# Graph layers on one core: in the second layer, one tile of rows in sixteen chunks fetched by SP row by row

## Chip, cores and metric

One of the eight cores of a Trainium2 chip runs the whole kernel. The metric is the device time of one execution in microseconds; before the change three runs took 8138.94, 8143.89 and 8145.72 us, median 8143.89 us.

## The reference

Twelve and a half thousand nodes of 128 numbers pass through two graph layers over 400,000 edges that are sorted by destination. The second layer is the one that the change touches:

```python
# layer 2, in the reference's own function _L1_gnn_ref(h, src, dst, etype, norm, W, b):
H = jnp.einsum('ni,rio->rno', h, W)
msg = (H[etype, src] + b[etype]) * norm
out = jax.ops.segment_sum(msg, dst, num_segments=h.shape[0])
return jax.nn.relu(out)
# and around it:
h = jnp.maximum(_layernorm(x, axis=-1), 0.0)
x = x + _L1_gnn_ref(h, src, dst, edge_type_8, edge_weight1, L1_gnn_W, L1_gnn_b)
```

The first layer runs a small network of two edge and two node products on each edge (source row, destination row, 64 edge features), sums the results by destination and adds them to the nodes.

## The kernel before, in words

**Tiling.** The edges are cut into 782 chunks of 512, each of four tiles (TC = 4) of 128 edges, one edge to a partition. Each layer goes over all chunks once (the number of passes is read from the data and is 1 here), with four slots of buffers (SL = 4): chunk c uses slot c modulo 4.

**Layer 2, engine by engine.** Each chunk passes through five queues, which meet on semaphores.

- SP (`layer1_pass`, line 495, its `step` at lines 496 to 500): waits until the chunk that last had the slot has been scattered, then loads the 128 x 4 source row numbers of the chunk (`idx`, line 500).
- POOL (`gather`, lines 542 to 552, called at line 594): waits for the same slot and for its `idx`, then issues four indirect DMAs (line 549), each of which fetches 128 rows of 512 bytes of the table `h_tab` into a tile of `rows` (in the profile `rows_place`).
- DVE (`build_hot1`, lines 931 to 962): builds for each tile the matrix that says to which of 32 nodes and 8 relations each edge adds, times its weight (line 959), and smaller ones (`hot`, `et_w`). `add_pair` (line 964) adds a pair's results into the accumulator `agg` (line 974).
- PE (`scatter`, lines 1123 to 1134): waits for DVE's matrices, for the rows (`rows_landed`) and for the bank; then four products of 128x128 by 128x256 (line 1130) and four small ones (line 1132). After both chunks of a pair `project` (lines 1136 to 1146) multiplies the sums of the pair before by the eight relation matrices (line 1143) and the bias (line 1145). The end of `scatter` is the semaphore `scattered[slot]`, for which SP, POOL and DVE wait.
- ACT (`copy_sums`, line 699): copies the sums of a chunk out of PSUM.

**Order.** The order on each engine is written out by hand. SP and POOL loop over four chunks at a time (`all_chunks`, line 333, with its loop at line 335), PE and DVE over two pairs (`paired`, line 287). A number that is read from memory into a register of an engine comes from `value_load`; in layer 1 SP does it once a chunk (`window_start`, line 370, the load itself line 371) for the first row of a window of `qr_tab`, which it then loads (line 476):

```python
def window_start(eng, c):
    return eng.value_load(base_i[0:1, ds(c.i, 1)], min_val=0, max_val=TOP)
...
start = window_start(sp, c)
sp.wait_ge(h2_summed[s], c.turn + 1)
hold(sp)
sp.dma_start(qr_w[s][:, :], qr_tab[:, ds(start, W), :]).then_inc(qr_landed[s], 16)
```

`hold` (line 362) puts an empty instruction behind a wait, so that the wait stands in an instruction of its own. In layer 2 SP reads nothing into registers inside the loop.

Of the kernel before, what the change touches and what calls it, by code (L numbers as in the profile page):

```python
# [23 lines left out]
def gnn_two_layers(nc, x, src_t, dst_t, etype_t, weight_t, dst_c, edge_cols,  # L24
# [3 lines left out]
    ds = bass.ds  # L28

    P = 128  # L30
# [4 lines left out]
    TC = 4  # L35
# [12 lines left out]
    TOP = NPAD - W  # L48
    KEY = W + 2
    EPS = 1e-5  # L50
    assert NG % 2 == 0 and NCH % 2 == 0 and NCH > 2 * SL and TC * H1 == P and 2 * H2 == P and 2 * EA == P and 3 * W <= P
    QP = max(q for q in range(1, P + 1) if NROW % q == 0)
    QC = NROW // QP
# [9 lines left out]
    with ctx:  # L63
        def sb(name, shape, dt=f32):
            return ctx.enter_context(nc.sbuf_tensor(name, shape, dt))

        def sem(name):
            return ctx.enter_context(nc.semaphore(name))

        def slot_sems(name, n=SL):  # L70
            return [sem(f"{name}{k}") for k in range(n)]
# [105 lines left out]
        h1_sb = sb("h1_sb", [P, P])  # L177
        h2_sb = sb("h2_sb", [P, 2 * P])
        tile_sums = sb("tile_sums", [P, D])

        bank = [ctx.enter_context(nc.psum_tensor(f"bank{k}", [P, 512], f32)) for k in range(8)]
        ps_h1, ps_msg1, ps_h2, ps_msg2, ps_tiles, ps_agg = bank[0:6]
# [48 lines left out]
        scattered, sums_copied = slot_sems("scattered"), slot_sems("sums_copied")  # L231
        projected, half_added, pair_added = slot_sems("projected", 2), sem("half_added"), slot_sems("pair_added", 2)
        pass1_ready, pass1_step = sem("pass1_ready"), sem("pass1_step")

        block = ctx.enter_context(nc.Block())

# [50 lines left out]
        def paired(m_, eng, step):  # L287

            L = (NPAIR - 2) // 2
            at = lambda i, quad=0: Pair(m_, quad + i // 2, i % 2)  # L290
            step(at(0), None, at(1))
            with eng.Fori(0, L) as quad:
                for i in range(1, 3):
                    step(at(i, quad), at(i - 1, quad), at(i + 1, quad))
            for i in range(2 * L + 1, NPAIR):
                step(at(i), at(i - 1), at(i + 1) if i + 1 < NPAIR else None)
            step(None, at(NPAIR - 1), None)

        class Group:

# [32 lines left out]
        def all_chunks(eng, m, step):  # L333

            with eng.Fori(0, NCH // SL) as quad:
                for u in range(SL):
                    step(Chunk(m, quad, u))
            for u in range(NCH % SL):
                step(Chunk(m, NCH // SL, u))
# [22 lines left out]
        def hold(eng):  # L362

            eng.nop(nofuse=True)

        def number_of_passes(eng):
            eng.wait_ge(passes_set, 1)
            return eng.value_load(passes_i[0:1, 0:1], min_val=1, max_val=MAXPASS)
# [20 lines left out]
        def _(sp):  # L389
# [103 lines left out]
            passes = number_of_passes(sp)  # L493

            def layer1_pass(m):
                def step(c):
                    s = c.slot
                    sp.wait_ge(scattered[s], c.turn + 1)
                    hold(sp)
                    sp.dma_start(idx[s][:, :], src_t[:, ds(c.i * TC, TC)]).then_inc(idx1_landed[s], 16)  # L500

                all_chunks(sp, m, step)


            with sp.Fori(0, passes) as m:
# [16 lines left out]
        def _(pool):  # L522
# [16 lines left out]

            pool.iota(pass_i[:, :], [[W, MAXPASS]], base=0, channel_multiplier=0).then_inc(ramps_set, 1)  # L540

            def gather(c, table, rows_of, used, idx_there, landed):
                s = c.slot
                pool.wait_ge(used[s], c.turn + 1)
                hold(pool)
                pool.wait_ge(idx_there[s], 16 * c.turn + 16)
                hold(pool)
                for t in range(TC):
                    pool.indirect_dma_start(  # L549
                        out=rows_of[s][:, t, :], out_offset=None, in_=table,  # L550
                        in_offset=bass.IndirectOffsetOnAxis(ap=idx[s][:, t:t + 1], axis=0),
                    ).then_inc(landed[s], 16)
# [37 lines left out]
            for b in range(2):  # L590
                pool.wait_ge(x_in_moved[b], 2 * MOVES)
            passes = number_of_passes(pool)
            with pool.Fori(0, passes) as m:
                all_chunks(pool, m, lambda c: gather(c, h_tab, rows, scattered, idx1_landed, rows_landed))


            with pool.Fori(0, NG // 2) as it:
# [404 lines left out]
        def _(pe):  # L1002
# [117 lines left out]

            def scatter(c):

                s = c.slot
                pe.wait_ge(hot1_built[s], c.turn + 1)
                pe.wait_ge(rows_landed[s], 16 * TC * c.turn + 16 * TC)
                pe.wait_ge(sums_copied[s], c.turn + 1)
                for t in range(TC):
                    pe.matmul(bank[s][:, 0:RW], rows[s][:, t, :], hot_rel[s % 2][:, t, :], start=(t == 0), stop=(t == TC - 1))  # L1130
                for t in range(TC):
                    ins = pe.matmul(bank[s][0:R, RW:RW + W], et_w[s][:, t, :], hot[s][:, t, :],  # L1132
                                    start=(t == 0), stop=(t == TC - 1))
                ins.then_inc(scattered[s], 1)
# [10 lines left out]
                pe.matmul(there, b_rel_sb[:, :], w_sums[p.half][:, :, :].rearrange("p c n -> p (c n)"), start=False, stop=True)\  # L1145
                  .then_inc(projected[p.half], 1)

            def step1(pair, before, after):
                if pair:
                    for c in pair.chunks:  # L1150
                        scatter(c)
                if before:
                    project(before)

            with pe.Fori(0, passes) as m:
                paired(m, pe, step1)


            all_groups(pe, lambda k: transpose_agg(k, k.it + NG // 2, (fin_even, fin_relu)))
# [56 lines left out]
```

## Time and profile before

| what | value |
|---|---|
| median of three runs | 8143.89 us |
| span of the profiled execution | 8149.0 us |
| PE busy | 84% |
| POOL busy | 75% |
| DVE busy | 49% |
| ACT busy | 24% |
| share of 16 DMA engines, layer 2 | about 0.21 |

The page gives no time of the profiled execution other than its span; the span is 5.1 us above the median of the runs. Layer 1 fills the stretch from about 150 to 4080 us, layer 2 from about 4180 to 8105 us. SP does no arithmetic, so the page has no busy time for it: its instructions are read from the view of a line and from the timeline, where "SPq" is SP's instruction queue. In the timeline a row is start, duration, engine, line, operation; the duration of a DMA on SPq is that of its issue, not of its transfer.

### The profile page before, as it was taken

The numbers are of one execution on the slowest core, as the hardware profiler recorded it, in microseconds if no ns is written. First come the engines' busy times: TensorE is split into PE (matmuls) and PEld (weight loads), VectorE is DVE, ScalarE is ACT, GpSimd is POOL, SyncE is SP. The second block draws the span as 40 slices with busy tenths as digits, with TensorE's granted clock in tenths as the row PEclk, the third lists the DMA queues.
The fourth block names the chain that finished last, engine by engine and source line by source line (L and its number), as shares of the span: only waits on it lengthen the run. The fifth ranks groups of instructions, "written<-read, shape, count | busy, mean of one in ns | idle before, by whom it ended". The sixth has DMA issues, their size and how long they took to land.

```text
span 8149.0 us, 187072 instructions
## 1 busy us (share of the span) xinstructions
PE 6825.6 (84%) x52884; PEld 5276.0 (65%) x52884; DVE 3995.9 (49%) x13480; ACT 1919.9 (24%) x4919; POOL 6074.5 (75%) x6335
## 2 busy tenths in 40 slices
PE   5999999999999999999967777777778877777777
PEld 4666666666666666666646666666666666666665
DVE  7333333333333333333365555555555556555554
ACT  2333333333333333333330000000000000000001
POOL 5777777777777777777757777777777777777776
PEclk7999999999999999999979888888888888988898
DMA  6333333333333333333322222222222222222222
GB/s 141 82 83 82 81 83 82 83 82 83 82 83 82 82 83 82 83 83 82 82 61 53 53 53 53 53 53 52 53 53 53 53 52 53 52 53 53 53 53 72
DMA packets 797549, 566.94 MB, mean 70 GB/s; under 512 B 481443, under 2 KB 671019, under 8 KB 797292
## 3 DMA queue, kind: packets, MB, share of 16 engines
q0 software_dynamic: 200192, 256.65, 14.6%
q1 hardware_dynamic: 597340, 310.10, 14.5%
q8 instruction: 6, 0.10, 0.0%
q14 instruction: 11, 0.09, 0.0%
HBM read 544.45 MB, written 21.68 MB: 69 GB/s over the span
## 4 chain that ended last, share of the span: by engine, by line
PE 32%; issue 24%; POOL 21%; DMA 20%; DVE 1%; POOLq 1%; SPq 0%; ACT 0%; DVEq 0%; ACTq 0%
PE bank L1130 19%; POOL shared L549 17%; DMA shared<-p_tab,idx 11%; DMA rows_place<-h_tab,idx 6%; PE bank L1143 5%; POOL rows_place L549 4%; PE bank L1132 3%; DMA idx<-in_src_t 2%; PE bank L1054 2%; PE bank L1145 1%; PE bank L1061 1%; PE bank L1080 0%; DMA x_in<-in_x 0%; PE bank L1071 0%; DVE stats L744 0%
## 5 line engine op out<-in xcount | busy, mean ns | idle before, releaser
L549 POOL DMA_INDIRECT shared<-p_tab,idx x3128 | 2984.1, 954 | 959.8 <-issue 826.7
L549 POOL DMA_INDIRECT rows_place<-h_tab,idx x3128 | 2978.3, 952 | 964.3 <-issue 804.4
L1130 PE MATMUL bank<-shared,rows_place 128*128 128x256 f32 x6256 | 1842.2, 446 | 860.4 <-issue 748.1
L1130 PEld LDWEIGHTS bank<-shared,rows_place 128*128 128x128 f32 x6256 | 1296.4, 218 | 1126.6 <-issue 782.8
L959 DVE TENSOR_SCALAR shared<-iota_key,key,w_f 128x256 f32<-128x256 f32 x3128 | 1139.1, 425 | 745.3 <-PE bank L1132 633.1
L704 ACT ACTIVATE x_in<-bank 128x256 f32<-128x256 f32 x782 | 300.8, 385 | 3591.9 <-PE bank L1132 3264.7
L1061 PE MATMUL bank<-h_sb,w_tile 128*128 128x128 f32 x6256 | 907.7, 288 | 22.3 <-DVE h_sb L870 0.8
L1061 PEld LDWEIGHTS bank<-h_sb,w_tile 128*128 128x128 f32 x6256 | 758.5, 191 | 232.4 <-DVE h_sb L870 232.1
L1080 PE MATMUL bank<-wn_half,h_sb 128*128 128x128 f32 x6256 | 890.3, 285 | 0.0
L870 DVE TENSOR_SCALAR h_sb<-bank 128x128 f32<-128x128 f32 x782 | 228.2, 292 | 1315.8 <-PE bank L1054 1294.3
L1143 PE MATMUL bank<-x_in,w_rel_sb 128*128 128x64 f32 x6256 | 862.8, 296 | 0.0
L1143 PEld LDWEIGHTS bank<-x_in,w_rel_sb 128*128 128x128 f32 x6256 | 807.0, 209 | 26.7
L880 DVE TENSOR_TENSOR shared<-bank,bn_rep 128x512 f32<-128x512 f32 x782 | 541.1, 692 | 539.7 <-PE bank L1080 534.2
L1080 PEld LDWEIGHTS bank<-wn_half,h_sb 128*128 128x128 f32 x6256 | 762.3, 192 | 0.0
L653 ACT ACTIVATE shared<-shared 128x512 f32<-128x512 f32 x782 | 493.4, 631 | 904.4 <-DVE shared L880 903.3
L649 ACT ACTIVATE shared<-bank,be_col 128x512 f32<-128x512 f32 x782 | 537.5, 687 | 708.2 <-PE bank L1061 708.2
L944 DVE TENSOR_SCALAR et_w<-iota_key,et_key,w_f 128x8 f32<-128x8 f32 x3128 | 695.0, 303 | 0.0
L1054 PE MATMUL bank<-ident,shared 128*128 128x128 f32 x1564 | 382.5, 326 | 292.5 <-DMA shared<-p_tab,idx 285.0
L1047 PEld LDWEIGHTS bank<-shared,w_pair 128*128 128x128 f32 x3128 | 408.4, 190 | 252.7 <-issue 239.9
L1047 PE MATMUL bank<-shared,w_pair 128*128 128x128 f32 x3128 | 557.5, 301 | 12.7 <-DMA shared<-in_edge_cols 12.7
L974 DVE TENSOR_TENSOR agg<-agg,bank 128x32 f32 x782 | 147.8, 189 | 815.2 <-PE bank L1145 498.0
L839 DVE SCALAR_TENSOR_TENSOR hot<-iota_f,base_c,dst_f 128x128 f32<-128x128 f32 x1564 | 538.0, 344 | 0.0
(105 smaller groups left out, 5379.0 us busy)
## 6 DMA issues: line engine op xcount, KB each, us to landing
rows_place<-in_dst_c SPq DMA_DIRECT2D x782, 192.0 KB
shared<-in_edge_cols SPq DMA_DIRECT2D x782, 128.0 KB
shared<-p_tab,idx POOLq DMA_INDIRECT x3128
rows_place<-h_tab,idx POOLq DMA_INDIRECT x3128
idx<-in_src_t SPq DMA_DIRECT2D x1564, 2.0 KB
qr_w<-qr_tab SPq DMA_DIRECT2D x782, 18.0 KB
x_in<-in_x SPq DMA_DIRECT2D x14, 448.0 KB, 4.7
h_tab<-x_in SPq DMA_DIRECT2D x14, 448.0 KB, 3.0
```

The source lines that it names most:

```text
L549: pool.indirect_dma_start(out=rows_of[s][:, t, :], out_offset=None, in_=table, in_offset=bass.IndirectOffsetOnAxis(ap=idx[s][:, t:t + 1], ...
L649: act.activation(msg1_sb[:, :], ps_msg1[:, :], ACT.Relu, bias=be2_col[:, 0:1]).then_inc(msg1_done, 1)
L839: return dve.scalar_tensor_tensor(out=hot[c.slot][:, :, :], in0=tiled(iota_f[:, 0:W], TC), scalar=base_c[:, ds(c.i, 1)], in1=wide(dst_f[:, ...
L880: dve.tensor_tensor(msg2_sb[:, :], ps_msg2[:, :], bn2_rep[:, :], ALU.add).then_inc(msg2_biased, 1)
L944: dve.tensor_scalar(et_w[c.slot][:, t, :], iota_key[:, :, 0], et_key[:, at], w_f[:, at], ALU.is_equal, ALU.mult)
L959: ins = dve.tensor_scalar(hot_rel[u % 2][:, t, :], iota_key[:, :, :].rearrange("p r n -> p (r n)"), key[k][:, n * TC + t:n * TC + t + 1], ...
L1047: pe.matmul(ps_h1[:, 0:P], w1_pair[:, q, :], ea[s][:, q * P:(q + 1) * P], start=(q == 0), stop=False)
L1054: pe.matmul(ps_h1[:, 0:P], prow[s][:, :, :].rearrange("p t o -> p (t o)"), ident[:, :], start=False, stop=True)\
L1061: ins = pe.matmul(ps_msg1[:, t * P:(t + 1) * P], w2_tile[:, t, :], h1_sb[:, :], start=True, stop=True)
L1080: ins = pe.matmul(ps_msg2[:, t * P:(t + 1) * P], h2_sb[:, b * P:(b + 1) * P], wn2_half[:, a, :], start=True, stop=True)
L1130: pe.matmul(bank[s][:, 0:RW], rows[s][:, t, :], hot_rel[s % 2][:, t, :], start=(t == 0), stop=(t == TC - 1))
L1143: pe.matmul(there, w_rel_sb[:, r, :], rel_sums[p.half][:, r, :, :].rearrange("p c n -> p (c n)"), start=(r == 0), stop=False)
```

## The change

Of the four tiles of chunk 13 of each 16 chunks in layer 2, POOL fetches three. SP fetches the first tile itself with 128 DMAs of one row each. It takes the row numbers of that tile into one partition (`row_ids`, one DMA per 16 chunks, loaded one group of 16 ahead), reads them into registers, 12 or 8 at a time, and issues 12 or 8 row DMAs behind the `idx` load of each of the first 13 chunks. The rows go to `single_rows`, two buffers in the space of `h`, and PE reads them in place of the chunk's first tile and waits for their semaphore besides. The loops of SP, POOL and PE in layer 2 are written out over 32 chunks, two groups of 16; 48 groups cover 768 chunks, and the last 14 chunks run as before.

```diff
--- before.py
+++ after.py
@@ -48,6 +48,9 @@
     TOP = NPAD - W
     KEY = W + 2
     EPS = 1e-5
+    SUP = 16
+    NSUP = NCH // SUP
+    SINGLE_AT = 13
     assert NG % 2 == 0 and NCH % 2 == 0 and NCH > 2 * SL and TC * H1 == P and 2 * H2 == P and 2 * EA == P and 3 * W <= P
     QP = max(q for q in range(1, P + 1) if NROW % q == 0)
     QC = NROW // QP
@@ -177,6 +180,8 @@
         h1_sb = sb("h1_sb", [P, P])
         h2_sb = sb("h2_sb", [P, 2 * P])
         tile_sums = sb("tile_sums", [P, D])
+        single_rows = h[0][:, 0:2, :]
+        row_ids = h[0][0:1, 2:4, :].bitcast(i32)
 
         bank = [ctx.enter_context(nc.psum_tensor(f"bank{k}", [P, 512], f32)) for k in range(8)]
         ps_h1, ps_msg1, ps_h2, ps_msg2, ps_tiles, ps_agg = bank[0:6]
@@ -231,6 +236,7 @@
         scattered, sums_copied = slot_sems("scattered"), slot_sems("sums_copied")
         projected, half_added, pair_added = slot_sems("projected", 2), sem("half_added"), slot_sems("pair_added", 2)
         pass1_ready, pass1_step = sem("pass1_ready"), sem("pass1_step")
+        row_ids_landed, single_landed = sem("row_ids_landed"), slot_sems("single_landed", 2)
 
         block = ctx.enter_context(nc.Block())
 
@@ -296,6 +302,35 @@
                 step(at(i), at(i - 1), at(i + 1) if i + 1 < NPAIR else None)
             step(None, at(NPAIR - 1), None)
 
+        SINGLE_ROWS = [12 if u % 2 == 0 and u < 12 else 8 for u in range(SINGLE_AT)]
+        assert sum(SINGLE_ROWS) == P and NSUP % 2 == 0 and NSUP * SUP + SINGLE_AT < NCH
+
+        class Single:
+
+
+            def __init__(self, m, two, half):
+                self.half, self.turn = half, m * (NSUP // 2) + two
+                self.k = two * 2 + half
+                self.ids_turn = m * (NSUP + 1) + self.k
+
+        def superchunks(eng, m, step):
+
+            with eng.Fori(0, NSUP // 2) as two:
+                for half in range(2):
+                    for u in range(SUP):
+                        step(Chunk(m, two * (2 * SUP // SL) + (half * SUP + u) // SL, u % SL), u, Single(m, two, half))
+            for u in range(NSUP * SUP, NCH):
+                step(Chunk(m, 0, u), None, None)
+
+        def tiles_gathered(c, u, single):
+
+            if c.slot != SINGLE_AT % SL:
+                return TC * c.turn + TC
+            before = c.m * (TC * SLOT_USES[c.slot] - NSUP)
+            if single is None:
+                return before + TC * (c.i // SL + 1) - NSUP
+            return before + single.k * (TC * SUP // SL - 1) + (TC * (u // SL + 1) - (u >= SINGLE_AT))
+
         class Group:
 
 
@@ -493,13 +528,31 @@
             passes = number_of_passes(sp)
 
             def layer1_pass(m):
-                def step(c):
+                def load_ids(k, half):
+                    sp.dma_start(row_ids[0:1, half, :], src_t[:, ds((k * SUP + SINGLE_AT) * TC, 1)].rearrange("p o -> o p"),
+                                 allow_slow_non_contiguous=True)\
+                      .then_inc(row_ids_landed, 16)
+
+                def step(c, u, single):
                     s = c.slot
                     sp.wait_ge(scattered[s], c.turn + 1)
                     hold(sp)
                     sp.dma_start(idx[s][:, :], src_t[:, ds(c.i * TC, TC)]).then_inc(idx1_landed[s], 16)
-
-                all_chunks(sp, m, step)
+                    if single is None:
+                        return
+                    if u == 0:
+                        sp.wait_ge(row_ids_landed, 16 * single.ids_turn + 16)
+                        hold(sp)
+                        load_ids(single.k + 1, 1 - single.half)
+                    if u < SINGLE_AT:
+                        first, n = sum(SINGLE_ROWS[:u]), SINGLE_ROWS[u]
+                        _, at = nc.values_load_multi_w_load_instructions(
+                            row_ids[0:1, single.half, first:first + n], engines=(sp.engine,), min_val=0, max_val=NPAD - 1)
+                        for p, row in zip(range(first, first + n), at):
+                            sp.dma_start(single_rows[p:p + 1, single.half, :], h_tab[ds(row, 1), :]).then_inc(single_landed[single.half], 16)
+
+                load_ids(0, 0)
+                superchunks(sp, m, step)
 
 
             with sp.Fori(0, passes) as m:
@@ -539,13 +592,13 @@
 
             pool.iota(pass_i[:, :], [[W, MAXPASS]], base=0, channel_multiplier=0).then_inc(ramps_set, 1)
 
-            def gather(c, table, rows_of, used, idx_there, landed):
+            def gather(c, table, rows_of, used, idx_there, landed, tiles=range(TC)):
                 s = c.slot
                 pool.wait_ge(used[s], c.turn + 1)
                 hold(pool)
                 pool.wait_ge(idx_there[s], 16 * c.turn + 16)
                 hold(pool)
-                for t in range(TC):
+                for t in tiles:
                     pool.indirect_dma_start(
                         out=rows_of[s][:, t, :], out_offset=None, in_=table,
                         in_offset=bass.IndirectOffsetOnAxis(ap=idx[s][:, t:t + 1], axis=0),
@@ -590,8 +643,12 @@
             for b in range(2):
                 pool.wait_ge(x_in_moved[b], 2 * MOVES)
             passes = number_of_passes(pool)
+
+            def step1(c, u, single):
+                gather(c, h_tab, rows, scattered, idx1_landed, rows_landed, range(1 if single and u == SINGLE_AT else 0, TC))
+
             with pool.Fori(0, passes) as m:
-                all_chunks(pool, m, lambda c: gather(c, h_tab, rows, scattered, idx1_landed, rows_landed))
+                superchunks(pool, m, step1)
 
 
             with pool.Fori(0, NG // 2) as it:
@@ -1120,14 +1177,18 @@
 
 
 
-            def scatter(c):
+            def scatter(c, u, single):
 
                 s = c.slot
                 pe.wait_ge(hot1_built[s], c.turn + 1)
-                pe.wait_ge(rows_landed[s], 16 * TC * c.turn + 16 * TC)
+                alone = single and u == SINGLE_AT
+                pe.wait_ge(rows_landed[s], 16 * tiles_gathered(c, u, single))
+                if alone:
+                    pe.wait_ge(single_landed[single.half], 16 * P * single.turn + 16 * P)
                 pe.wait_ge(sums_copied[s], c.turn + 1)
                 for t in range(TC):
-                    pe.matmul(bank[s][:, 0:RW], rows[s][:, t, :], hot_rel[s % 2][:, t, :], start=(t == 0), stop=(t == TC - 1))
+                    there = single_rows[:, single.half, :] if alone and t == 0 else rows[s][:, t, :]
+                    pe.matmul(bank[s][:, 0:RW], there, hot_rel[s % 2][:, t, :], start=(t == 0), stop=(t == TC - 1))
                 for t in range(TC):
                     ins = pe.matmul(bank[s][0:R, RW:RW + W], et_w[s][:, t, :], hot[s][:, t, :],
                                     start=(t == 0), stop=(t == TC - 1))
@@ -1145,15 +1206,25 @@
                 pe.matmul(there, b_rel_sb[:, :], w_sums[p.half][:, :, :].rearrange("p c n -> p (c n)"), start=False, stop=True)\
                   .then_inc(projected[p.half], 1)
 
-            def step1(pair, before, after):
+            def step1(pair, before, u, single):
                 if pair:
-                    for c in pair.chunks:
-                        scatter(c)
+                    for k, c in enumerate(pair.chunks):
+                        scatter(c, u + k if single else None, single)
                 if before:
                     project(before)
 
+            PAIRS = SUP // 2
+
             with pe.Fori(0, passes) as m:
-                paired(m, pe, step1)
+                at = lambda i, two=0: Pair(m, two * PAIRS + i // 2, i % 2)
+                step1(at(0), None, 0, Single(m, 0, 0))
+                with pe.Fori(0, NSUP // 2) as two:
+                    for i in range(1, 2 * PAIRS + 1):
+                        ahead, half, u = i // (2 * PAIRS), i // PAIRS % 2, i % PAIRS * 2
+                        step1(at(i, two), at(i - 1, two), u, Single(m, two + ahead, half))
+                for i in range(NSUP * PAIRS + 1, NPAIR):
+                    step1(at(i), at(i - 1), None, None)
+                step1(None, at(NPAIR - 1), None, None)
 
 
             all_groups(pe, lambda k: transpose_agg(k, k.it + NG // 2, (fin_even, fin_relu)))
```

## Rows read from the trace of the kernel before

**Rows 1.** The page: busy time of each engine and its share of the span.

```profile
PE 6825.6 (84%) x52884; PEld 5276.0 (65%) x52884; DVE 3995.9 (49%) x13480; ACT 1919.9 (24%) x4919; POOL 6074.5 (75%) x6335
```

**Rows 2.** Busy time by stretch: layer 1, then layer 2.

```profile
core 0: us, PE busy (x) PEld busy (x) DVE busy (x) ACT busy (x) POOL busy (x), PEclk, DMA share, GB/s
200.00:4200.00 4000.00, 3623.81 (x32679) 2729.44 (x32678) 1561.38 (x4198) 1493.84 (x3232) 2990.13 (x3127) 0.99 0.35 82
4400.00:8000.00 3600.00, 2829.62 (x17913) 2247.06 (x17911) 2108.56 (x8248) 323.40 (x1434) 2726.79 (x2865) 0.89 0.21 53
```

**Rows 3.** Groups of instructions in layer 2, 4300 to 8100 us.

```profile
L549 POOL DMA_INDIRECT rows_place<-h_tab,idx x3023 | 2878.4, 952 | 921.7 <-issue 775.1 <-PE bank L1132 120.1 <-DMA idx<-in_src_t 26.5
L1130 PE MATMUL bank<-shared,rows_place 128*128 128x256 f32 x6048 | 1776.3, 445 | 810.5 <-issue 725.2 <-DMA rows_place<-h_tab,idx 85.3
L959 DVE TENSOR_SCALAR shared<-iota_key,key,w_f 128x256 f32<-128x256 f32 x3024 | 1101.8, 425 | 718.8 <-PE bank L1132 609.0 <-issue 45.2 <-DVE key L947 39.4
```

**Rows 4.** Timeline of POOL in the middle of layer 2: start, duration, operation, idle before.

```profile
6024.15 0.95 POOL L549 DMA_INDIRECT rows_place<-h_tab,idx  x1 [0.31 <-issue]
6025.40 0.97 POOL L549 DMA_INDIRECT rows_place<-h_tab,idx  x1 [0.30 <-issue]
6026.67 0.95 POOL L549 DMA_INDIRECT rows_place<-h_tab,idx  x1 [0.30 <-DMA idx<-in_src_t]
6027.93 0.95 POOL L549 DMA_INDIRECT rows_place<-h_tab,idx  x1 [0.31 <-issue]
```

**Rows 5.** Chain of waits in layer 2, 5997 to 6030 us: start, duration, what.

```profile
6000.41 3.48 PE bank L1130 x8
...
6004.23 1.93 PE bank L1143 x16
6006.16 0.36 PE bank L1145 x2
...
6012.76 2.63 DMA rows_place<-h_tab,idx
...
6015.44 1.99 PE bank L1130 x8
6017.43 0.33 PE bank L1132 x8
```

**Rows 6.** What SP waits for over the span: us in total, times, longest.

```profile
SPq L364 <- PE bank L1132: 3083.5, 700, 12.4
```

**Rows 7.** SP's instructions of the `idx` load, layer 2: ns min/median/max.

```profile
L500 SPq DMA_DIRECT2D idx<-in_src_t x753: 288/333/343, 4302.7 to 8083.6; - x189
L500 SPq FUSED_REGOPS  x751: 46/46/46, 4302.5 to 8075.0; - x188
L500 SPq MOVE idx<-in_src_t x751: 29/29/29, 4302.6 to 8075.1; - x188
```

**Rows 8.** SP reading one number into a register, layer 1 (`window_start`).

```profile
L371 SPq TENSOR_LOAD <-base_i x782: 292/432/461, 144.6 to 4067.1; - x196
L371 SPq FUSED_REGOPS  x782: 159/168/178, 145.0 to 4067.6; - x196
L371 SPq SEQ_ASSERT  x782: 18/26/26, 145.2 to 4067.8; - x196
```

**Rows 9.** Timeline of SP in layer 1: DMAs with addresses from registers.

```profile
206.06 0.35 SPq L466 DMA_DIRECT2D idx<-in_src_t  x1
206.59 0.33 SPq L467 DMA_DIRECT2D shared<-in_edge_cols  x1
```

**Rows 10.** Timeline of SP at the start: DMAs with fixed addresses, back to back.

```profile
3.85 0.43 SPq L400 DMA_DIRECT2D bias_node<-in_bn  x1
4.32 0.43 SPq L401 DMA_DIRECT2D agg<-in_dst_c  x1
```

**Rows 11.** The same: one row to one partition, then rows to 128 partitions.

```profile
54.34 0.22 SPq L437 DMA_DIRECT2D agg<-range_d  x1
54.61 0.35 SPq L438 DMA_DIRECT2D base<-base_d  x1
```

**Rows 12.** The load of `qr_w` on SP, 200 to 2200 us: a DMA in three parts.

```profile
L476 SPq DMA_DIRECT2D qr_w<-qr_tab x398: 813/823/837, 199.7 to 2198.1; - x199
```

**Rows 13.** DMA issues: KB each, median us from issue to landing.

```profile
base_d<-least SPq DMA_DIRECT2D x1, 3.1 KB, 1.6
```

## The prediction

> **What bounds the kernel now.** I read the page first, then the stretches, then the groups of layer 2, then the timeline of POOL there. The page alone misleads: over the span PE is the busiest engine and POOL is at three quarters [rows 1]. The change touches layer 2 only, so the question is what sets the pace there. The stretches show PE at 2829.62 of 3600 us (79%) and POOL at 2726.79 (76%) [rows 2], neither full. The groups settle it: POOL's gathers are busy for 2878.4 us and idle for 921.7 before them, which is the whole stretch of 3800 us, and 775.1 us of that idle time is "issue", time in which POOL waits for nothing that the profile shows [rows 3]. The timeline shows why: a gather of 0.95 us, 0.30 us of issue, the next gather, even where a wait is named as the cause [rows 4]. So a gather costs 3800 / 3023 = 1.257 us of POOL, four make a chunk of 5.03 us, and 16 chunks take 80.4 us. **POOL sets the pace of layer 2, gather after gather.** PE has room: two scatters of 1.99 + 0.33 and one project of 1.93 + 0.36 are 6.9 us [rows 5] in a pair of chunks that lasts 10.05. DVE waits for PE's scatters for 609.0 us of this stretch [rows 3]. SP waits for scatters nearly all the time, 3083.5 us in 700 recorded waits [rows 6].
>
> **What is removed.** One gather in 64: 48 of them, POOL's 1.257 us each, on the path. If nothing else became late, 48 x 1.257 = 60 us would go (80.4 us per 16 chunks becomes 79.2).
>
> **What is added on SP, per 16 chunks.** SP must do all of the following within 79.2 us, or the `idx` loads that stand in the same queue come late and POOL waits for them.
>
> The gap between two instructions of SP is about 0.04 us: two back-to-back DMAs with fixed addresses start 0.47 apart and take 0.43 [rows 10].
>
> (a) One row DMA with its row number in a register. Its address needs register arithmetic and a move ahead of it. In layer 1 two such DMAs start 0.53 us apart, of which the first one's issue is 0.35 [rows 9], so the surroundings of one are 0.18 us. The issue itself: a DMA of one row to one partition took 0.22 us, and its neighbour to 128 partitions 0.35 [rows 11]; the steady `idx` load takes 0.333 [rows 7]. A one-row DMA is nearest to the first, so I take 0.22, sum 0.40 us; the other end is 0.333 + 0.18 = 0.51.
>
> (b) The check of each row number. The change reads its numbers with a minimum and a maximum, as `window_start` does, and there each of 782 loaded numbers is followed by register arithmetic of 0.168 us and an assertion of 0.026 [rows 8]. With a gap for each that is 0.27 us. I assume that it comes once per number also where 8 or 12 are read together, since each has to be compared. The other end is that many numbers share one check, next to nothing.
>
> One row is thus 0.40 + 0.27 = 0.67 us, and 128 rows are **86 us: more than the 79.2 us that there are**, before SP has done anything else.
>
> (c) Reading the numbers. One number takes 0.432 us [rows 8]. Thirteen reads at 0.47 are 6.1 us if all 8 or 12 come at the price of one; if a read brings four numbers, 32 reads are 15 us. I take the first as the cheaper reading of the same row.
>
> (d) Sixteen `idx` loads as before: 0.046 + 0.029 + 0.333 us [rows 7], the wait ahead and the gaps, 0.58 us each, 9.3 us.
>
> (e) One load of 128 single numbers into one partition: between 0.333 [rows 7] and 0.823, the dearest DMA of SP [rows 12]; I take 0.6 and its wait, 0.7 us.
>
> (f) A pause once per 16 chunks. Behind chunk 12 there are no rows, so SP issues the loads of chunks 13, 14 and 15 at once and then waits until chunk 12 is scattered. From its `idx` load that takes about 1.6 us to land [rows 13], four gathers of 1.257, 2.63 us for the last rows [rows 5] and a scatter of 2.3, together 11.5 us. SP fills 0.6 + 0.5 + 8 x 0.67 + 3 x 0.58 = 8.2 of them. Pause 3.3 us. Between ends of nothing and 5.
>
> Sum of SP: 86 + 6.1 + 9.3 + 0.7 + 3.3 = **105.4 us** per 16 chunks against 80.4 now: 25.0 us more, 48 times, 1200 us. Against the profiled span: 8149 + 1200 = 9349 us; the median of the runs lies 5 us below the span, so 9344.
>
> The Trainium skill (Runtime: NRT & Kernel Launch, section "Instruction fetch mechanics") puts a load into registers at about 200 ns for each register even in bulk. By that part (c) would be 26 us and the time some 950 us longer; the one-number load here, 0.432 us [rows 8], neither confirms nor excludes it.
>
> **What lies beside other work.** The transfers of the rows: 128 x 512 bytes are the same bytes that the gather moved, and the DMA engines are at 0.21 of their time in layer 2 [rows 2]; I cost them at nothing, and with SP this slow they are spread over 86 us. PE's new wait for the single rows costs nothing either: the last row DMA is issued ahead of the `idx` load of chunk 13, whose gathers then still have to run. If that cover were gone, PE would be held by at most one landing, about 2 us per 16 chunks, which four slots of buffers absorb. What is queued behind SP's row DMAs is the next `idx` load, in the first 13 steps of 16; POOL waits for that, and behind POOL everything.
>
> **Rivals.**
>
> 1. *SP keeps up* (the other side: faster). If the numbers are read without a check of each, a row is 0.40 us and SP needs 51 + 6.1 + 9.3 + 0.7 = 67 us, less than 79.2. Then POOL still sets the pace and the gain is 60 us: 8144 - 60 = 8084 us. For it: SP has been idle nearly throughout [rows 6]. Against it: 782 checks for 782 numbers [rows 8]. The point from which it decides is a row price of (79.2 - 16.1) / 128 = 0.49 us; mine is 0.67. Chance 0.12. The Trainium skill (DMA: Bandwidth & Descriptors, section "Issuing engines are not separate DMA queues") says that issuing from a further engine saves only the sequencer's time to start a DMA, which is usually small beside the DMA; read so, SP's issue would not matter and this rival would hold. The rows show 0.22 to 0.35 us of issue for one DMA [rows 11] against 1.257 us for a gather that brings 128 rows [rows 3].
>
> 2. *SP keeps up, but POOL loses the gain in its long loop.* The loop body becomes eight times longer; if each of the 24 returns to its top cost POOL about as much as two gathers, 2.5 us, the 60 us would be gone: 8144 us. Nothing in the trace speaks for it, since the loops of four chunks show no such stop [rows 4]. Chance 0.03.
>
> 3. *SP is the bound and dearer.* Issue at 0.333 instead of 0.22 adds 14 us per 16 chunks, reading four at a time 9 us; together 23 x 48 = 1100 us, 10450 us. Chance 0.25 for landing beyond 9900.
>
> 4. *PE's clock falls.* With SP the bound, a pair lasts 105.4 / 8 = 13.2 us and PE works 6.9 of it. In layer 2 the granted clock is 0.89 and not 0.99 as in layer 1, where PE is busy 91% [rows 2], and a scatter at the lower level took 3.48 in place of 1.99 us [rows 5]. All at half speed, a pair would need 13.8 us, 110 us per 16 chunks, and PE would take over: 9570 us. This lies inside the forecast's own range.
>
> **How the numbers follow.** Slower 0.85: it includes rivals 3 and 4. Faster 0.12, no change 0.03; 0.2% (16 us) is about what a measurement of this kernel tells from none. The likeliest is SP at 105 us, 9344 us. The low end: the gaps between instructions may be narrower when no profile is taken; a row has five of them, and at half their width it is 0.57 us, SP's sum 92 us and the time some 8700; I go to 8600. The high end is rival 3 with a little of rival 4, 10600. Beyond the two ends stay rivals 1 and 2 and some 5 in 100 above.
>
> **What the profile would show.** In layer 2, POOL's idle time ends on the `idx` load instead of "issue", with 20 to 30 us more of it per 16 chunks, and its gathers keep 0.95 us each, 3080 of them. SP has 6144 row DMAs, with as many assertions. Waits of SP for scatters shrink from most of the layer to a few us per 16 chunks. Right for (a): row DMAs about 0.22 us long and, without the checks, 0.40 apart; for (b): arithmetic of 0.17 us and an assertion per row; for (c): 13 reads per 16 chunks. The forecast is wrong if SP's row DMAs follow each other at under 0.49 us, checks included, or if SP still waits for scatters for 10 us or more in each 16 chunks.

## The result, and the profile after

The changed kernel takes 9787.61 us (median of four runs, 9787.24 to 9793.34) against 8141.68 us before (four runs, 8138.94 to 8145.72): 1.2024 times as long, 95% interval 1.2009 to 1.2038. **It is slower by 1646 us, 34.3 us in each of the 48 groups of 16 chunks.** The forecast was 9344 us, slower, with a range of 8600 to 10600.

The page of the changed kernel: span, busy time, instruction loads, and the chain that ended last by engine and by line. The profiled execution took 9787.24 us for a span of 9785.4.

```profile
span 9785.4 us, 217607 instructions
PE 7349.9 (75%) x52884; PEld 5612.0 (57%) x52884; DVE 3968.0 (41%) x13480; ACT 1919.9 (20%) x4919; POOL 6018.1 (62%) x6287
q14 instruction: 325, 2.66, 0.1%
SPq 36%; issue 27%; POOL 16%; DMA 13%; PE 5%; DVE 1%; POOLq 0%; ACT 0%; ACTq 0%; DVEq 0%
SPq L552 18%; SPq L549 15%; POOL shared L602 15%; DMA shared<-p_tab,idx 9%; DMA idx<-in_src_t 3%; SPq L540 3%; PE bank L1191 2%; PE bank L1111 1%; POOL rows_place L602 1%; DMA rows_place<-h_tab,idx 1%; SPq L532 0%; PE bank L1118 0%; DMA x_in<-in_x 0%; PE bank L1204 0%; PE bank L1137 0%
```

No compute engine has a larger share of the span than before [rows 1]; PE's busy time alone grew, by 524 us (see rival 4 below). The chain of work that ended last now runs through SP's queue for 36% of the span: line 552 is the row DMA, line 549 the reading and checking of row numbers. The stretch of layer 2 that answers to [rows 2], the groups of POOL and PE beside those of [rows 3] (here from the page, so for the whole of layer 2), and POOL's timeline beside [rows 4]:

```profile
4400.00:8000.00 3600.00, 2328.91 (x12600) 1796.56 (x12600) 1465.87 (x5789) 226.92 (x1006) 1881.05 (x1981) 0.76 0.15 37
```

```profile
L602 POOL DMA_INDIRECT rows_place<-h_tab,idx x3080 | 2926.4, 950 | 2657.1 <-DMA idx<-in_src_t 1872.0
L1191 PE MATMUL bank<-shared,rows_place 128*128 128x256 f32 x6160 | 2287.4, 535 | 1869.5 <-issue 971.4
```

```profile
5011.95 0.94 POOL L602 DMA_INDIRECT rows_place<-h_tab,idx  x1 [0.30 <-issue]
5015.41 0.94 POOL L602 DMA_INDIRECT rows_place<-h_tab,idx  x1 [2.52 <-DMA idx<-in_src_t]
5016.65 0.94 POOL L602 DMA_INDIRECT rows_place<-h_tab,idx  x1 [0.30 <-issue]
5017.90 0.94 POOL L602 DMA_INDIRECT rows_place<-h_tab,idx  x1 [0.30 <-issue]
5019.15 0.94 POOL L602 DMA_INDIRECT rows_place<-h_tab,idx  x1 [0.30 <-issue]
5024.86 0.94 POOL L602 DMA_INDIRECT rows_place<-h_tab,idx  x1 [4.78 <-DMA idx<-in_src_t]
```

In 3600 us POOL starts 1981 gathers instead of 2865. A gather costs what it did, 0.94 us and 0.30 of issue, but after each four POOL stops for 2.5 or 4.8 us until the next `idx` has landed: 1872.0 us over the whole layer. The DMA engines are less used than before: 0.15 of their time and 37 GB/s, against 0.21 and 53 [rows 2]. Why `idx` is late is seen in SP's timeline, which starts one step earlier (line 552 row DMAs, line 540 `idx`):

```profile
5005.77 0.36 SPq L540 DMA_DIRECT2D idx<-in_src_t  x1
5009.11 3.14 SPq L552 DMA_DIRECT2D h<-h_tab  x8
5012.60 0.36 SPq L540 DMA_DIRECT2D idx<-in_src_t  x1
5017.48 4.74 SPq L552 DMA_DIRECT2D h<-h_tab  x12
5022.47 0.36 SPq L540 DMA_DIRECT2D idx<-in_src_t  x1
5025.81 3.15 SPq L552 DMA_DIRECT2D h<-h_tab  x8
5029.36 0.36 SPq L540 DMA_DIRECT2D idx<-in_src_t  x1
5033.93 1.11 SPq L552 DMA_DIRECT2D h<-h_tab  x3
```

Two `idx` loads are 6.8 us apart with 8 rows between them and 9.9 with 12; POOL wants one in 5.0. Almost half of such a step shows no DMA at all: from the end of `idx` at 5022.83 to the first row at 5025.81 are 2.98 us, and with 12 rows (5029.72 to 5033.93) 4.21. That is the reading and checking. SP's instructions in it, and those of the DMAs, over the whole kernel (ns min/median/max):

```profile
L549 SPq FUSED_REGOPS  x6144: 147/147/183, 4163.3 to 9646.7; - x199
L549 SPq SEQ_ASSERT  x6144: 18/18/24, 4163.5 to 9646.9; - x199
L549 SPq TENSOR_LOAD <-h x624: 705/724/1241, 4162.5 to 9644.1; - x156
```

```profile
L552 SPq FUSED_REGOPS  x6144: 37/37/48, 4166.3 to 9649.8; - x199
L552 SPq MOVE h<-h_tab x6144: 29/29/38, 4166.4 to 9649.9; - x199
L552 SPq DMA_DIRECT2D h<-h_tab x6144: 219/228/341, 4166.5 to 9650.0; - x199
```

There are as many checks as rows, 6144, and 624 reads, 13 to a group. What SP waits for in layer 2 (4300 to 9700 us; us in total, times, longest), beside [rows 6]:

```profile
SPq L399 <- PE bank L1193: 146.7, 45, 8.0
```

SP, which waited for scatters nearly all the time, now waits once in a group, for 3 us. It has become the bound.

Summed over SP's records from 4387 to 9523 us (5744 rows, 44.9 groups), each with the gap behind it, a group costs (the parts add up to the elapsed time whatever they are, so the table shows where SP's time goes; that SP sets the pace is for the experiments to show):

| term | forecast, us | measured, us |
|---|---|---|
| (a) issue of 128 rows | 51 | 54.3 |
| (b) check of 128 numbers | 35 | 33.2 |
| (c) 13 reads | 6.1 | 11.5 |
| (d) 16 `idx` loads | 9.3 | 10.4 |
| (e) the row numbers' load | 0.7 | 0.95 |
| (f) pause behind chunk 12 | 3.3 | 2.8 |
| return of the loop | not priced | 1.4 |
| sum | 105.4 | 114.4 |

### The profile page after: what moved, and what is told of

It is laid out like the page before. It is cut to its first block, busy times and chain, and to the rows that moved or that the text cites. A ratio compares the mean times of both kernels' runs of the same rounds, so it can differ in the third digit from the quotient of the medians.

```text
span 9785.4 us, 217607 instructions
## 1 busy us (share of the span) xinstructions
PE 7349.9 (75%) x52884; PEld 5612.0 (57%) x52884; DVE 3968.0 (41%) x13480; ACT 1919.9 (20%) x4919; POOL 6018.1 (62%) x6287
## 4 chain that ended last, share of the span: by engine, by line
SPq 36%; issue 27%; POOL 16%; DMA 13%; PE 5%; DVE 1%; POOLq 0%; ACT 0%; ACTq 0%; DVEq 0%
SPq L552 18%; SPq L549 15%; POOL shared L602 15%; DMA shared<-p_tab,idx 9%; DMA idx<-in_src_t 3%; SPq L540 3%; PE bank L1191 2%; PE bank L1111 1%; POOL rows_place L602 1%; DMA rows_place<-h_tab,idx 1%; SPq L532 0%; PE bank L1118 0%; DMA x_in<-in_x 0%; PE bank L1204 0%; PE bank L1137 0%
## 5 line engine op out<-in xcount | busy, mean ns | idle before, releaser
L602 POOL DMA_INDIRECT rows_place<-h_tab,idx x3080 | 2926.4, 950 | 2657.1 <-DMA idx<-in_src_t 1872.0
L1191 PE MATMUL bank<-shared,rows_place 128*128 128x256 f32 x6160 | 2287.4, 535 | 1869.5 <-issue 971.4
L1191 PEld LDWEIGHTS bank<-shared,rows_place 128*128 128x128 f32 x6160 | 1581.8, 269 | 2253.0 <-issue 990.8
L1016 DVE TENSOR_SCALAR shared<-iota_key,key,w_f 128x256 f32<-128x256 f32 x3128 | 1115.9, 419 | 2385.2 <-PE bank L1193 2203.6
L1128 PE MATMUL bank<-shared,wn_msg 128*64 128x256 f32 x3128 | 513.7, 405 | 0.8 <-ACT shared L706 0.8
```

What stands on the lines that cost most here:

```text
L602: pool.indirect_dma_start(out=rows_of[s][:, t, :], out_offset=None, in_=table, in_offset=bass.IndirectOffsetOnAxis(ap=idx[s][:, t:t + 1], ...
L1016: ins = dve.tensor_scalar(hot_rel[u % 2][:, t, :], iota_key[:, :, :].rearrange("p r n -> p (r n)"), key[k][:, n * TC + t:n * TC + t + 1], ...
L1191: pe.matmul(bank[s][:, 0:RW], there, hot_rel[s % 2][:, t, :], start=(t == 0), stop=(t == TC - 1))
```

## The experiments

The theory: SP's own instruction time sets the pace of layer 2, so that time follows that sum, and POOL's pace (80.4 us with four gathers a chunk, 79.2 with one less in 16) is the floor. Rivals, that is other possible causes of the longer time: the loops of 32 chunks, the one-row transfers or PE's wait for them, POOL or the DMA engines, and uneven steps. Times are medians, ratios those to the kernel before on the same chip (median 8141.93 us for the first four, 8144.16 for the next four, 8139.35 for the last two). Each diff is against the changed kernel, and "..." stands for lines left out.

**e1, the long loops alone.** No row work on SP; POOL fetches all four tiles.

```diff
-                    if u == 0:
-                        sp.wait_ge(row_ids_landed, 16 * single.ids_turn + 16)
-                        hold(sp)
-                        load_ids(single.k + 1, 1 - single.half)
-                    if u < SINGLE_AT:
...
-                gather(c, h_tab, rows, scattered, idx1_landed, rows_landed, range(1 if single and u == SINGLE_AT else 0, TC))
+                gather(c, h_tab, rows, scattered, idx1_landed, rows_landed, range(TC))
...
```

> The changed kernel with its loops written out over 32 chunks, but no row work: POOL fetches all four tiles, SP only loads idx. Theory 'SP's own instruction time sets the pace': SP needs 10 us of the 80.4 per 16 chunks, so POOL sets it again and the time is that of the kernel before, 8144 us within 0.3%. Rival 'the long loops cost it' (code fetched again at each return and every so many instructions, on POOL, PE or SP): most of the 1640 us stays, at least 8300 us.

Measured 8143.05 us, ratio 0.9998 (0.9989 to 1.0008). The loops of POOL and PE, eight times as long, cost nothing; behind the branch at its return POOL stops for 0.22 us. That rival is out, and rival 2 of the prediction with it. SP's own loop is short in this run, so of its length e1 says nothing.

**e4, reading and checking without the row DMAs.** POOL fetches all four tiles.

```diff
-                        for p, row in zip(range(first, first + n), at):
-                            sp.dma_start(single_rows[p:p + 1, single.half, :], h_tab[ds(row, 1), :]).then_inc(single_landed[single.half], 16)
...
```

> The changed kernel in which SP reads and checks all 128 row numbers but issues no row DMA; POOL fetches all four tiles. Theory SP's instruction time: SP needs 128 x 0.252 = 32 + 11.5 + 9.6 + 0.8 + 2 = 56 us per 16 chunks, hidden behind POOL's 80.4: 8144 us within 0.3%. If reading numbers from SBUF into registers disturbed something by itself (a stall of SP that grows, a slower POOL): clearly more, 8300 us and up.

Measured 8141.5 us, ratio 0.9999 (0.9990 to 1.0009). This part of SP's new work is hidden entirely.

**e5, the row DMAs without reading and checking.** The row numbers are constants, the first 128 rows of the table each time. The kernel leaves out the load of the row numbers, their reading and check and the address arithmetic, and so adds up wrong rows for that tile: the run measures time alone. The true rows at the same pace come in e10.

```diff
...
-                            sp.dma_start(single_rows[p:p + 1, single.half, :], h_tab[ds(row, 1), :]).then_inc(single_landed[single.half], 16)
+                            sp.dma_start(single_rows[p:p + 1, single.half, :], h_tab[p:p + 1, :]).then_inc(single_landed[single.half], 16)
...
```

> The changed kernel with 128 one-row DMAs per 16 chunks at fixed rows of the table: no row numbers are loaded, read or checked (layer 2 then adds up wrong rows for that tile, with the same work on every engine). Theory SP's instruction time: 128 x 0.27 = 35 us + 10 us for idx, 45 of 79 us, hidden even in the 12-row steps; the removed gather then shows: 8142 - 60 = 8082 us (0.9926). Rival 'the one-row transfers or PE's wait for them cost something themselves': above that; at 8142 they would eat the gather's whole worth.

Measured 8081.2 us, ratio 0.9930 (0.9916 to 0.9943): 63 us under the kernel before, where 48 gathers of 1.257 us are 60. So the removed gathers are worth what the prediction gave them, and 6144 one-row transfers, PE's wait for them and steps of 12 and 8 cost nothing, as long as SP has the time. Each half of the new work alone is free (e4, e5); together they are not.

**e3, the gather put back.** SP does all its row work, POOL fetches the tile as well; PE still uses SP's rows.

```diff
...
-                gather(c, h_tab, rows, scattered, idx1_landed, rows_landed, range(1 if single and u == SINGLE_AT else 0, TC))
+                gather(c, h_tab, rows, scattered, idx1_landed, rows_landed, range(TC))
```

> The changed kernel with POOL's removed gather put back (POOL fetches all four tiles of each chunk; PE still uses SP's rows). Theory SP's instruction time: POOL has 30 us to spare per 16 chunks, so the gather that was removed is worth nothing now: 9788 us within 0.3%. A theory in which POOL or the DMA engines still share the bound gives 48 x 1.257 = 60 us more, 9848 us.

Measured 9790.72 us, ratio 1.2018 (1.1998 to 1.2039), beside 9787.61 for the changed kernel. POOL has so much time left that the removed gathers gain nothing.

**e9, 104 rows instead of 128.** Eight in each of the 13 steps; POOL fetches all four tiles and PE uses them.

```diff
-        SINGLE_ROWS = [12 if u % 2 == 0 and u < 12 else 8 for u in range(SINGLE_AT)]
+        SINGLE_ROWS = [8] * SINGLE_AT
...
```

> SP fetches 104 rows per 16 chunks, checked, 8 in each of 13 steps; POOL fetches all four tiles and PE uses POOL's, only waiting for SP's. Theory SP's instruction time, with prices from the changed kernel's trace: 104 x 0.684 = 71.1, 13 reads x 0.745 = 9.7, idx 10.4, row numbers' load 0.95, loop return 1.4, sum 93.6, with the pause 96.4 us per 16 chunks against 80.4: 8142 + 16 x 48 = 8910 us; 8775 if the pause is no cost of its own. A theory in which the fourth tile's way through SP (PE's use of it, its landing) costs, not SP's time: 8142.

Measured 8985.15 us, ratio 1.1035 (1.1018 to 1.1052). The cost grows with the number of rows: 17.6 us a group over the kernel before with 104, 34.3 with 128. The expectation was 75 us too low, 1.6 us a group; in its trace a row costs 0.69 us, and SP's waits for scatters are 177.9 us from 4300 to 8900 us, nearly 4 a group.

**e6, even steps.** Eight rows in each of 16 steps, the first 24 of a tile behind chunks 13 to 15 of the group before.

```diff
...
                     if u < SINGLE_AT:
-                        first, n = sum(SINGLE_ROWS[:u]), SINGLE_ROWS[u]
...
+                        fetch_rows(single.half, EARLY + STEP_ROWS * u, STEP_ROWS)
+                    else:
...
+                        fetch_rows(1 - single.half, STEP_ROWS * (u - SINGLE_AT), STEP_ROWS)
...
```

> The changed kernel with 8 rows in each of 16 steps (the next tile's first 24 rows are fetched behind chunks 13 to 15) in place of 12 and 8 in 13 steps; checks kept. Theory: SP has the same instructions but one, 16 x (8 x 0.66 + 0.75 + 0.60) = 106 us, 0.8 for the row numbers' load and 3 us of code fetching: 110 us per 16 chunks; the pause of 3 to 4 us behind chunk 12 goes. 9565 us, some 220 below the changed kernel. If the pause was no cost of its own: 9788.

Measured 9737.14 us, ratio 1.1962 (1.1944 to 1.1981): 50 us less than the changed kernel, where 220 were expected. The trace has no wait of SP left, so the pause (f), 2.8 us a group, is gone; but over half of it comes back (a group lasts 113.2 us in this trace, not 111.6): 16 reads cost 12.2 instead of 11.5 us, and the rest is spread over rows and `idx` loads. I had also carried over too low prices: 0.60 for `idx`, where its steps take 0.68, and 0.66 for a row, where it takes 0.686.

**e2, no check.** One argument more in the reading of the row numbers: the numbers of `src` are node numbers, all below the table's end.

```diff
-                            row_ids[0:1, single.half, first:first + n], engines=(sp.engine,), min_val=0, max_val=NPAD - 1)
+                            row_ids[0:1, single.half, first:first + n], engines=(sp.engine,), min_val=0, max_val=NPAD - 1,
+                            skip_runtime_bounds_check_because="src holds node numbers alone, all below NPAD")
```

> The changed kernel with the range check of each row number left out, all else the same, the row DMAs too. Theory SP's instruction time: one row costs 0.406 us instead of 0.66, SP's sum per 16 chunks is 52 + 11.5 (register loads) + 9.6 (idx) + 0.8 + 2.3 (code) = 76 us, under POOL's 79.2, so POOL sets the pace: 8084 us if nothing leaks, up to 8200 because the 12-row steps last 6.4 us against 5.0 and SP lags some us within each 16 chunks. Rival 'the 128 one-row transfers or PE's wait for them hurt': no change from 9788. Rival long loops: no large change.

Measured 8325.6 us, ratio 1.0232 (1.0215 to 1.0249). The check was worth 1462 us; 48 x 33.2 us would be 1594, and most of the rest was lost again in SP's waits for scatters, 2.8 us a group before and some 5 now. And 184 us over the kernel before remain, outside the expected 8084 to 8200. The waits of SP and POOL, 4300 to 8000 us (in total, times, longest):

```profile
POOL rows_place L603 <- DMA idx<-in_src_t: 260.3, 205, 2.7
SPq L399 <- PE bank L1194: 222.4, 80, 5.1
```

Both wait, by turns: SP's instructions are some 78.6 us a group in this trace, just under POOL's 79.2, and a group lasts 84.0. In its 13 steps with rows SP falls behind POOL; behind chunk 12 it could catch up, but the slots let it run only four chunks ahead, so it waits some 5 us there for scatters, and the time is lost. That is argued from the waits; e7 puts it to the test.

**e7, even steps and no check** (e6 with the argument of e2).

> e6 without the range checks. Theory: a step of SP is 8 x 0.406 + 0.75 + 0.60 = 4.6 us and with code fetching 4.75, under POOL's 4.95 per chunk; nothing accumulates over 13 steps as in e2: POOL sets the pace, 8082 to 8110 us, faster than the kernel before. If e2's remaining 184 us came from something other than its uneven steps (an average SP load too near POOL's pace, the DMAs), e7 stays above 8200.

Measured 8120.01 us, ratio 0.9973 (0.9963 to 0.9984): **faster than the kernel before**, by 0.3% and clear of the noise, and e2's remaining 184 us were indeed the uneven steps. It stays 10 us above the expected range. SP's waits, 4300 to 8000 us:

```profile
SPq L399 <- PE bank L1208: 3.4, 3, 2.7
```

SP never rests: its instructions sum to 79.6 us a group, 54.4 of them rows at 0.425 each, 12.2 reads, 10.7 `idx`. It is still the bound, by a hair over POOL's 79.2. In e5 the same row of this view has 1249.1 us of waiting.

**e8, rows shared between SP and ACT, checks kept.** SP fetches 64 rows in 12 steps of 8, 4, 4; ACT the other 64, eight behind each pair's copies, one group ahead.

```diff
...
+        def fetch_rows(eng, half, first, n):
+            _, at = nc.values_load_multi_w_load_instructions(
+                row_ids[0:1, half, first:first + n], engines=(eng.engine,), min_val=0, max_val=NPAD - 1)
+            for p, row in zip(range(first, first + n), at):
+                eng.dma_start(single_rows[p:p + 1, half, :], h_tab[ds(row, 1), :]).then_inc(single_landed[half], 16)
...
+                    if 0 < u < SINGLE_AT:
...
+                        fetch_rows(sp, single.half, first, n)
...
+                        copy_sums(Pair(m, two * (SUP // 2) + i // 2, i % 2))
...
+                        fetch_rows(act, 1 - half, HALF_TILE + 8 * j, 8)
...
```

> The changed kernel with the 128 rows shared: SP 64 in 12 steps of 8, 4, 4, ACT 64 in steps of 8 behind each pair's copies, checks kept on both. Theory 'an issuing engine's instruction time': SP 64 x 0.66 + 6.4 + 9.6 + 2 = 60 us, ACT 42 + 6 + 9 = 57 us per 16 chunks, both under 79: POOL sets the pace, 8082 to 8100 us. If ACT's copies of the sums, now queued behind up to 6 us of DMA issues, hold up PE and the slots: above 8142.

Measured 8095.16 us, ratio 0.9944 (0.9930 to 0.9957): faster than the kernel before with every check in place. All 6144 rows and their checks are there (and 64 of each more, ACT's last step ahead, which nobody uses), but on two queues (SPq and ACTq in this view of the line; ns min/median/max):

```profile
L319 ACTq FUSED_REGOPS  x3136: 147/147/172, 4166.2 to 7983.4; - x196
L319 SPq FUSED_REGOPS  x3072: 147/147/176, 4166.1 to 7955.2; - x192
L319 SPq TENSOR_LOAD <-h x576: 481/497/794, 4165.5 to 7953.8; - x192
L319 ACTq TENSOR_LOAD <-h x386: 713/724/2249, 4164.1 to 7981.1; - x193
```

**e10, shared and no check** (e8 with the argument of e2).

> e8 without the range checks on SP and ACT. Theory: e8 still lies 14 us above e5 because of steps in which SP or ACT is late for a moment; without checks SP needs about 45 and ACT 45 us per 16 chunks: 8082 us, as e5. If the 14 us come from something that the checks have no part in (DMA issues on ACT ahead of its copies, the transfers): 8095 as before.

Measured 8076.44 us, ratio 0.9925 (0.9911 to 0.9938), the lowest median of all, though its interval overlaps those of e5 and e8. POOL is back where it was before the change: 899.4 us idle in the 3700 from 4300 us, 771.4 of them "issue".

```profile
L611 POOL DMA_INDIRECT rows_place<-h_tab,idx x2950 | 2801.3, 950 | 899.4 <-issue 771.4 <-PE bank L1213 94.5 <-DMA idx<-in_src_t 33.6
```

## Why the prediction was right, and where it was off

The direction, the mechanism and the range held: a row at 0.67 us (0.684 measured), 128 of them more than POOL's 79.2 us, SP the bound, `idx` late, POOL waiting for it.

*What bounds the kernel, and what is removed.* Right: e5 shows the 60 us of the gathers by themselves, e3 that they are worth nothing once SP is the bound.

*(a) and (b), issue and check.* Both right in size, 86 us against 87.5; two small misses partly cancel (issue 3.3 us too low, check 1.8 too high). The nearest row for a one-row DMA, 0.22 us to one partition [rows 11], was the right one (0.228), and the check comes once per number, though 8 or 12 are read together. e2 takes it away and e4 shows that it costs nothing alone. The check was dearer in [rows 8] (0.168 and 0.026 us) than here (0.147 and 0.018).

*(c), the step that was off.* I took one read of 8 or 12 numbers at the price of a read of one, 0.432 us. It takes 0.705 with eight and 0.934 with twelve in the stretch from 5022 to 5034 us, where one of each stands (ns min/median/max):

```profile
L549 SPq TENSOR_LOAD <-h x2: 705/820/934, 5022.9 to 5029.8; - x2
```

That makes 11.5 us a group and not 6.1, 5.4 of the 9.0 us that were missing. My other end, 15 us, lay nearer. The Trainium skill's figure (Runtime: NRT & Kernel Launch, "Instruction fetch mechanics"), some 200 ns for each register, would have given an estimate of 26 us and is not what these reads from SBUF show. From one to four, eight and twelve numbers they take 0.432 [rows 8], 0.497 (e8), 0.705 and 0.934 us, so 0.05 to 0.06 us for each further one from four on. The count is not the whole of it: in e4, where no row DMAs stand ahead of the reads, the same two kinds take 0.527 and 0.752 us (medians), 8.6 us a group in place of 11.5:

```profile
L544 SPq TENSOR_LOAD <-h x624: 520/534/783, 4158.2 to 7993.4; - x156
```

So 0.19 us of each read come only with the row DMAs; why is open.

*The code of the long loop*, which I did not price on SP. The chain at the return of SP's loop, start, duration, what:

```profile
5070.96 0.33 SPq L540
5071.49 2.56 issue
5074.04 0.16 SPq L318
...
5084.52 0.40 issue
5084.92 0.23 SPq L552
```

Each of the 24 returns costs SP 2.6 us, and some 0.3 us go about every 19 us besides (the lower pair). Instructions being fetched is the reading that fits: the short stops come every 128 instructions of SP, a packet of 8192 bytes starts on queue 14 within 2 us behind each of the eleven between 5080 and 5290 us, one starts inside the long stop (at 5072.36), and the page counts 325 such packets. ACT, whose loop is long in e8, stops for 2.5 us too. In e1, whose SP loop is short, the gap behind the branch is 0.23 us and not 2.5, and the page says:

```profile
q14 instruction: 16, 0.13, 0.0%
```

In the changed kernel it is 1.4 us a group for the return and some 1.7 in the rows. Of POOL I had said that nothing in the trace speaks for such a stop; on POOL there is none (e1).

*(f), the pause.* Right in place and size (3.3 against 2.8 us), but e6 shows that little is won by filling it.

*The low end* rested on narrower gaps between instructions in runs without a profile. It fell: the other three runs took 9787.39 to 9793.34 us beside the profiled 9787.24.

*Rival 1, SP keeps up.* Its condition was a check not made. e2 makes that case, and the 8084 us that I gave it were wrong: SP then needs some 78.6 us and not 67, and loses 5 more to its uneven steps. The point at which it decides lies below the 0.49 us a row that I worked out, since the other terms are larger than I had them: in e7 0.425 is still too much by 0.4 us a group. The Trainium skill's rule (DMA: Bandwidth & Descriptors, "Issuing engines are not separate DMA queues"), that the issue is usually small beside the DMA, does not hold for a DMA of one row here. Between 5026 and 5030 us the queue of SP moved eight rows, in 16 packets:

```profile
q1 hardware_dynamic: 16, 0.00, 0.4%
```

That is 0.4% of the time of 16 engines in 4 us, some 0.03 us a row, where address and issue hold SP for 0.42. The packets start some 0.9 us behind their issue, but the rows follow each other every 0.41 us, so this time overlaps and the issue adds up. For the 128 rows of a tile SP pays 54.3 us of issue, POOL 1.257 us for the gather.

*Rival 3, SP dearer.* It did not come: the issue took 0.228 us and not 0.333, and 9788 us lie below the 9900 that it was to pass.

*Rival 4, PE's clock.* The granted clock, a mean of its full and its half level, fell from 0.89 to 0.76 in layer 2 (about half of the stretch after 4400 us stood at the half level), and a product of line 1191 took 535 ns on average in place of 445 [rows 3]. It did not set the pace: PE was busy for 65% of the 3600 us after 4400, and its scatters held up nobody for long (SP 74.3 us, POOL 1.2 us in the 3700 from 4300).

*The signs.* Gathers, row DMAs, assertions and SP's few waits came as forecast. POOL's idle time on `idx` did not: 20 to 30 us more a group were expected, and the page has 39 (1872.0 / 48), since the group grew by 34 us instead of 25 and the 0.30 us of issue ahead of a delayed gather count in it.

Not settled: the 14 us by which e8 lies above e5, hardly more than the noise of either (their intervals overlap). In e10 they are gone, which points at the checks; on which of the two queues they would arise wasn't tried.

## What to carry to other kernels

An engine that only issues DMAs has a budget too: its instructions per period, each with its gap, must fit into the period of the engine that waits for it, before any of its transfers count. A row whose number comes from memory costs reading, check, address and issue, so price all four; then spread the issues evenly over the steps and over two queues (e8 against the change: the same rows, 1692 us less). If half of a new load is free and the other half too, that says nothing on both together.

## What the hardware showed that I had not expected

A bounds check of one number in a register costs SP 0.26 us with its gaps (147 ns of arithmetic, 18 ns of assertion), about as much as the issue of a one-row DMA itself (0.228 us, 0.28 with its gap). Reading numbers from SBUF into registers is cheap in bulk, 0.497 us for four and 0.705 for eight, and cheaper without row DMAs ahead (0.527 for eight, e4). SP stops for 2.6 us at each return of a loop body of some 1450 instructions, while the 32-chunk loops of PE and POOL show no such cost (e1).
